# Four attention layers with a feed-forward: weighings in pairs, a rounded second product, shuffles out of PSUM, other places in the slots

## The reference

```python
# L0: layer norms, heads of 16, biases; then a feed-forward
x = x + softmax((ln(x) wq + bq)(ln(c) wk + bk)^T / 4) (ln(c) wv + bv) wo + bo
x = x + gelu(ln2(x) w1 + b1) w2 + b2            # 256 -> 1024 -> 256, exact gelu
# L1: heads of 64, rms norm of x, raw context, no scale
x = x + softmax((x * rsqrt(mean(x^2) + 1e-6) * nw wq)(c wk)^T) (c wv) wo
# L2: heads of 64, rotary embedding on q and k (pairs of neighbouring rows), mask, then layer norm
x = ln(x + softmax(where(mask, rope(x wq) rope(c wk)^T / 8, -1e9)) (c wv) wo) * gamma + beta
# L3: as L0, without the feed-forward
```

## Time and profile before

| | |
|---|---|
| median of three runs | 2268.0 us (2266.34 to 2273.81) |
| profiled execution, own time | 2268.11 us |
| its span | 2266.2 us |
| busy in the span: PE, PEld, DVE, ACT, POOL | 2062.2, 1678.8, 1425.7, 1263.5, 581.4 us |
| mean granted clock of TensorE | 0.963 |

### The profile page before, as it was taken

How to read it: one execution, slowest core, us unless ns; L and a number is a source line. 1 busy time by engine, 2 the same in 40 slices (tenths; PEclk the granted TensorE clock), 3 DMA queues, 4 the chain that set the end, 5 groups by cost and what they waited for, 6 DMA issues and landing times. The chain is left out here.

```text
span 2266.2 us, 50658 instructions
## 1 busy us (share of the span) xinstructions
PE 2062.2 (91%) x18696; PEld 1678.8 (74%) x18696; DVE 1425.7 (63%) x2880; ACT 1263.5 (56%) x3225; POOL 581.4 (26%) x676
## 2 busy tenths in 40 slices
PE   6888986979999999999989999899999998889897
PEld 5777775867787787787767777777777776777776
DVE  5777774335445455454587777777777775577775
ACT  3677774335555555555555555555555554577775
POOL 3232320000000000000055655655556551000000
PEclk8999997989999999999999999999999999799999
DMA  6444332011000000000001000000000000344432
GB/s 170 135 136 139 117 122 82 0 52 58 14 8 8 14 8 15 8 8 14 9 15 35 15 9 9 9 9 15 9 9 10 1 1 1 115 121 121 121 122 71
DMA packets 72965, 109.69 MB, mean 48 GB/s; under 512 B 7062, under 2 KB 62618, under 8 KB 72730
## 3 DMA queue, kind: packets, MB, share of 16 engines
q1 hardware_dynamic: 72442, 105.98, 15.4%
q10 hardware_dynamic: 288, 0.51, 0.1%
HBM read 69.28 MB, written 37.19 MB: 47 GB/s over the span
## 5 line engine op out<-in xcount | busy, mean ns | idle before, releaser
L1444 ACT ACTIVATE wide_P<-PS,MX 100x361 f32<-100x361 f32 x512 | 288.9, 564 | 415.3 <-DVE MX L1562 411.4
L1562 DVE TENSOR_REDUCE MX<-PS 100x2 f32<-100x722 f32 x256 | 231.5, 904 | 181.4 <-PE PS L1312 181.3
L626 ACT ACTIVATE L_P<-PS,MX 100x361 f32<-100x361 f32 x512 | 253.5, 567 | 132.2 <-DVE MX L752 132.2
L752 DVE TENSOR_REDUCE MX<-PS 100x2 f32<-100x722 f32 x256 | 219.9, 900 | 48.3 <-PE PS L512 47.7
L1738 POOL TENSOR_TENSOR wide_AC<-wide_T,wide_COSM 128x362 f32<-128x362 f32 x128 | 118.0, 922 | 409.4 <-DVE wide_SH L1520 408.1
L1335 PE MATMUL PS<-wide_PT,wide_V 128*64 128x100 f32 (+1 forms) x3072 | 189.1, 257 | 29.6 <-issue 29.6
L524 PE MATMUL PP<-CON,L_P 100*128 100x100 f32 x1536 | 183.9, 257 | 26.6 <-DVE L_PT L759 20.7
L1335 PEld LDWEIGHTS PS<-wide_PT,wide_V 128*64 128x64 f32 (+1 forms) x3072 | 139.4, 136 | 84.4 <-issue 68.2
L524 PEld LDWEIGHTS PP<-CON,L_P 100*128 100x128 f32 x1536 | 151.5, 144 | 47.8 <-ACT L_P L626 34.3
L1321 PE MATMUL PP<-CON,wide_P 100*128 100x100 f32 x1536 | 179.6, 254 | 0.8 <-ACT wide_PT L1451 0.5
L1321 PEld LDWEIGHTS PP<-CON,wide_P 100*128 100x128 f32 x1536 | 164.6, 144 | 10.4 <-issue 2.0
(11 more groups left out here) (255 smaller groups left out, 5434.4 us busy)
## 6 DMA issues: line engine op xcount, KB each, us to landing
strips<-L_KS SPq DMA_DIRECT2D x256, 90.5 KB
L_KA<-strips SPq DMA_DIRECT2D x64, 362.0 KB, 3.1
C<-ctx_t SPq DMA_DIRECT2D x32, 361.0 KB, 3.1
kept<-L_CTH SPq DMA_DIRECT2D x16, 361.0 KB, 4.9
kept<-L_CTL SPq DMA_DIRECT2D x16, 361.0 KB, 5.5
L_CTH<-kept SPq DMA_DIRECT2D x16, 361.0 KB, 4.3
L_CTL<-kept SPq DMA_DIRECT2D x16, 361.0 KB, 5.1
C<-in_ctx SPq DMA_DIRECT2D x16, 256.0 KB, 3.4
```

What stands on the lines that cost most here:

```text
L626: nc.scalar.activation(P[:, (4 * g + j) % 8, 0:SK], PSB[0:SQ, j, 0:SK], ACT.Exp, bias=MX[:, s % 2, 4 * q + j:4 * q + j + 1], scale=1.0).th ...
L752: nc.vector.tensor_reduce(MX[:, s % 2, 4 * q + 2 * i:4 * q + 2 * i + 2], PSB[0:SQ, 2 * i:2 * i + 2, 0:SK], AX.X, ALU.max, negate=True).the ...
L1444: nc.scalar.activation(P[:, (2 * g + i) % 4, 0:SK], PS_[i][0:SQ, 0:SK], ACT.Exp, bias=MX[:, s % 2, h:h + 1], scale=1.0, accum_out=DEN[:, s ...
L1562: nc.vector.tensor_reduce(MX[:, s % 2, 2 * p:2 * p + 2], PSB[0:SQ, 0:2, 0:SK], AX.X, ALU.max, negate=True).then_inc(Z["maxed"], 1)
```

## The change

- Narrow layers: ScalarE does job M ahead of the exponentials, VectorE job O ahead of the unload.
- Feed-forward: the output product is made transposed and in rounded halves (w2 and the hidden units split), unit by unit, two units behind the hidden product, with the bias b2 at the eviction; its result is turned back by TensorE. w1 is split in two parts. The loop is written out.
- Wide layers: one tile C for the raw context in place of two, so context s + 1 is loaded when that of s is split, and the first of these loads comes after those of L2's weights; the wait for w_o moves to the first projection. PT has six parts. Weighings g - 3 and g - 2 run together in odd slots. O moves from slot 3 to 5, V from slots 3, 4, 5 (and 5, 6, 7 behind the weighing) to 2, 3, 4 and 6, 7, 0.
- L2: VectorE swaps rows out of the PSUM bank, for keys right after the maximum; ScalarE's copy waits for the swap and GpSimd for the copy. The layer norm moves from slots 4 and 6 to 6 and 7. L2's output weights are loaded one entry later in SP's list.

The core of the diff (`turn`, `gain`, `stats`, `split` and `add` of the feed-forward are as before but for their indices; indentation is reduced):

```diff
-C = sb("C", [128, 2, KV_TILES, E])
+C = sb("C", [128, KV_TILES, E])
...
+        for key in a_:
+            if key[0] == "M":
+                job(key)
...
             exponential(g, 1)
         for key in a_:
-            job(key)
+            if key[0] != "M":
+                job(key)
...
         for key in a_:
-            if key[0] == "N":
+            if key[0] in "NO":
                 job(key)
         if turns:
             unload(g - 1)
         for key in a_ + b_:
-            if key[0] != "N":
+            if key[0] not in "NO":
...
+W1H, W1L = local("W1H", [128, KE, FF], f32r), local("W1L", [128, KE, FF], f32r)
+W2H, W2L = local("W2H", [128, nf, E], f32r), local("W2L", [128, nf, E], f32r)
...
+    def hidden(u):
+        i, t = divmod(u, nf)
+        pe.wait_ge(Z["w1_low"], 1 + 2 * t // nf)
+        pe.wait_ge(Z["y_low"], KE * (i + 1))
+        if u >= 2:
+            pe.wait_ge(Z["hid_taken"], u - 1)
+        c = slice(128 * t, 128 * t + 128)
+        todo = [x for k in range(KE) for x in ((W1H[:, k, c], YH[:, i % 2, k, :]), (W1H[:, k, c], YL[:, i % 2, k, :]),
+                                               (W1L[:, k, c], YH[:, i % 2, k, :]))]
+        for m, (x, y) in enumerate(todo):
+            last = nc.tensor.matmul(hid[u % 2][:, 0:GS], x, y, start=m == 0, stop=m == len(todo) - 1)
+        last.then_inc(Z["hid_made"], 1)
+    def output(u):
+        i, t = divmod(u, nf)
+        pe.wait_ge(Z["w2_low"], 1)
+        pe.wait_ge(Z["hid_low"], u + 1)
+        if t == 0 and i >= 2:
+            pe.wait_ge(Z["out_taken"], KE * (i - 1))
         for k in range(KE):
+            c = slice(128 * k, 128 * k + 128)
+            for m, (x, y) in enumerate(((W2H, HH), (W2H, HL), (W2L, HH))):
+                last = nc.tensor.matmul(outs[i % 2][k][:, 0:GS], x[:, t, c], y[:, u % 4, :], start=t == 0 and m == 0,
+                                        stop=t == nf - 1 and m == 2)
+        last.then_inc(Z["out_made"], 1)
...
+    def back(i, half):
+        pe.wait_ge(Z["out_taken"], KE * (i + 1))
+        if i + 2 < groups:
+            pe.wait_ge(Z["gained"], KE * (i + 2) + half + 1)
+        else:
+            pe.wait_ge(Z["added"], G * (i - 1) + 2 * half + 2)
+        for v in range(2):
+            g = 2 * half + v
+            for k in range(KE):
+                last = nc.tensor.transpose(turns[half][0:SQ, E * v + 128 * k:E * v + 128 * k + 128],
+                                           OT[:, k, SQ * g:SQ * g + SQ], ident)
+        last.then_inc(Z["back_made"], 1)
+    for k in range(KE):
+        turn(0, k)
+    for u, i, t in stream():
+        if u < U:
+            hidden(u)
+        if u >= 2:
+            output(u - 2)
+        if i + 1 < groups and t in (3, 4):
+            turn(i + 1, t - 3)
+        if 0 < i < groups and t in (5, 6):
+            back(i - 1, t - 5)
+    for half in range(2):
...
+    def split_w1(n):
+        act.wait_ge(w_in["ffn"][0], 16)
+        nc.scalar.activation(W1H[:, :, HALVES[n]], w1[:, :, HALVES[n]], ACT.Copy).then_inc(Z["w1_high"], 1)
...
+    def hidden(u):
+        act.wait_ge(Z["hid_made"], u + 1)
+        if u >= 3:
+            act.wait_ge(Z["hid_low"], u - 2)
+        nc.scalar.activation(H32[:, u % 3, :], hid[u % 2][:, 0:GS], ACT.Gelu, bias=col("b1", u % nf)).then_inc(Z["hid_taken"], 1)
+        act.wait_ge(Z["hid_taken"], u + 1)
+        if u >= 4:
+            act.wait_ge(Z["out_made"], u - 3)
+        nc.scalar.activation(HH[:, u % 4, :], H32[:, u % 3, :], ACT.Copy).then_inc(Z["hid_high"], 1)
+    def output(i):
+        act.wait_ge(Z["out_made"], nf * (i + 1))
+        if i:
+            act.wait_ge(Z["back_made"], 2 * i)
         for k in range(KE):
+            nc.scalar.activation(OT[:, k, :], outs[i % 2][k][:, 0:GS], ACT.Identity, bias=col("b2", k), scale=1.0).then_inc(Z["out_taken"], 1)
+    split_w1(0)
+    split_w1(1)
+    for k in range(KE):
+        gain(0, k)
+    act.wait_ge(wo_in["ffn"], 16)
+    nc.scalar.activation(W2H[:, :, :], w2, ACT.Copy).then_inc(Z["w2_high"], 1)
+    for u, i, t in stream():
+        if u < U:
+            hidden(u)
+        if i and t == 2 and i < groups:
+            output(i - 1)
+        if i + 1 < groups and t in (3, 4):
+            gain(i + 1, t - 3)
+    output(groups - 1)
...
+    def split_w1(n):
+        dve.wait_ge(Z["w1_high"], n + 1)
+        nc.vector.tensor_tensor(W1L[:, :, HALVES[n]], w1[:, :, HALVES[n]], W1H[:, :, HALVES[n]].bitcast(fp32),
+                                ALU.subtract).then_inc(Z["w1_low"], 1)
...
+    def hidden(u):
+        dve.wait_ge(Z["hid_high"], u + 1)
+        if u >= 4:
+            dve.wait_ge(Z["out_made"], u - 3)
+        nc.vector.tensor_tensor(HL[:, u % 4, :], H32[:, u % 3, :], HH[:, u % 4, :].bitcast(fp32), ALU.subtract).then_inc(Z["hid_low"], 1)
...
+    stats(0)
+    moments(0)
+    split_w1(0)
     normalise(0)
+    split_w1(1)
+    for k in range(KE):
+        split(0, k)
+    dve.wait_ge(Z["w2_high"], 1)
+    nc.vector.tensor_tensor(W2L[:, :, :], w2, W2H[:, :, :].bitcast(fp32), ALU.subtract).then_inc(Z["w2_low"], 1)
+    for u, i, t in stream():
+        if u < U:
+            hidden(u)
+        if i + 1 < groups:
+            if t == 0:
+                stats(i + 1)
+            elif t == 1:
+                moments(i + 1)
+            elif t == 2:
+                normalise(i + 1)
+            elif t in (4, 5):
+                split(i + 1, t - 4)
+        if 0 < i < groups and t in (5, 6):
+            add(i - 1, t - 5)
...
-after_scores, after_turn, after_weigh = [], [], []
+after_scores, after_turn = [], []
 if s + 1 < NS:
     after_scores.append(("K", s + 1, p))
 if s % 2 and s + 1 < NS:
...
     after_turn.append(("X", s + 2, 0))
 if p == 1 and s > 0:
     after_turn.append(("R", s - 1, 1))
-if p == 3 and s > 0:
+if p == 5 and s > 0:
     after_turn.append(("O", s - 1, 0))
 if p == 5 and s < NS:
     after_turn.append(("R", s, 0))
-if p in (3, 4, 5) and s < NS:
-    after_turn.append(("V", s, 3 + p - 3))
-if p in (5, 6, 7) and s + 1 < NS:
-    after_weigh.append(("V", s + 1, p - 5))
-return after_scores, after_turn, after_weigh
-
-SLOTS = [(s, p) for s in range(NS) for p in range(HP)] + [(NS, p) for p in range(4)]
+if p in (2, 3, 4) and s < NS:
+    after_turn.append(("V", s, 3 + p - 2))
+if p in (6, 7) and s + 1 < NS:
+    after_turn.append(("V", s + 1, p - 6))
+if p == 0 and 0 < s < NS:
+    after_turn.append(("V", s, 2))
+return after_scores, after_turn
+SLOTS = [(s, p) for s in range(NS) for p in range(HP)] + [(NS, p) for p in range(6)]
...
     context(0)
-    context(1)
...
-        if s + 2 < NS:
+        if s + 1 < NS:
             sp.wait_ge(Z["c_low"], KE * (s + 1))
-            context(s + 2)
+            context(s + 1)
...
+        if s == B + 1:
             sp.wait_ge(Z["added"], B)
...
         pe.wait_ge(Z["scaled"], 2 * (s + 1))
+        if s == 0:
+            pe.wait_ge(wo_in["L1"], 16)
...
-                                        PT[0:r, (2 * g + i) % 4, SQ * c:SQ * c + SQ], start=c == 0, stop=c == KV_TILES - 1)
+                                        PT[0:r, (2 * g + i) % 6, SQ * c:SQ * c + SQ], start=c == 0, stop=c == KV_TILES - 1)
...
-    pe.wait_ge(wo_in["L1"], 16)
...
-        if 2 <= g <= HP * NS + 1:
+        if g % 2 and 3 <= g <= HP * NS + 1:
+            weigh(g - 3)
             weigh(g - 2)
-        for key in after_weigh:
-            job(key)
...
-        act.wait_ge(Z["made"], job_no[key] + 1)
+        act.wait_ge(Z["shuffled"], r + 1)
         if r >= NT:
             act.wait_ge(Z["rotated"], r - NT + 1)
...
-        if g >= 2:
-            act.wait_ge(Z["weighed"], g - 1)
-        nc.scalar.activation(PT[:, (2 * g + 1) % 4, :], PP[1][:, 0:KV_TILES * SQ], ACT.Copy).then_inc(Z["unloaded_odd"], 1)
+        if g >= 3:
+            act.wait_ge(Z["weighed"], g - 2)
+        nc.scalar.activation(PT[:, (2 * g + 1) % 6, :], PP[1][:, 0:KV_TILES * SQ], ACT.Copy).then_inc(Z["unloaded_odd"], 1)
...
-        dve.wait_ge(Z["copied"], r + 1)
-        nc.vector.stream_shuffle(SH[:, r % NB, 0:n], T32[:, r % NT, 0:n], [q ^ 1 for q in range(32)]).then_inc(Z["shuffled"], 1)
+        dve.wait_ge(Z["made"], job_no[key] + 1)
+        nc.vector.stream_shuffle(SH[:, r % NB, 0:n], bank(key)[:, 0:n], [q ^ 1 for q in range(32)]).then_inc(Z["shuffled"], 1)
...
+        shuffles_first = s + 1 < NS and rope(s + 1)
+        if shuffles_first:
+            for key in after_scores:
+                job(key)
...
-        for key in after_scores:
-            job(key)
+        if not shuffles_first:
+            for key in after_scores:
+                job(key)
...
-            if p == 4 and s < NS:
+            if p == 6 and s < NS:
                 post_stats(s - 1)
-            if p == 6 and s < NS:
+            if p == 7 and s < NS:
                 post(s - 1)
...
-        pool.wait_ge(Z["shuffled"], r + 1)
+        pool.wait_ge(Z["copied"], r + 1)
...
-        if B < s < NS and p == 4:
+        if B < s < NS and p == 6:
```

(4 more changed lines are left out.)

241 lines of the change are left out of this document (97 added, 144 removed).

## The result

Median 2114.7 us (2111.77 to 2117.97) against 2270.7 us in the same runs: a ratio of 0.9315, interval 0.9291 to 0.9338, faster. The forecast was 2127 us, its range 2080 to 2185. Executed again among the last experiments, the changed kernel took 2118.1 us (2111.56 to 2119.25), ratio 0.9331 (0.9311 to 0.9352).

The account below looks back on a forecast made before the run. TensorE was taken as the busiest engine in every stage, short of work in different ways. Terms -38 (narrow layers), -17 (feed-forward), -2 (wide start), -24 (L1), -60 (L2) sum to -141: 2266.2 - 141 + 1.9 = 2127 us, range 2080 to 2185.

Parts of the forecast that it names:

- Narrow layers, -38: L0 and L3: moving job M's copy and job O's addition earlier returns two thirds of 57.8 us of weight-load waits.
- Feed-forward and start, -19 together: Feed-forward -17 from a cheaper second product and earlier row statistics; start of the wide layers -2.
- L1, -24: First wide layer: -19 from weighing in pairs, -5 from moving value products and O; ends -12 and -32.
- The pairs' step: Wide layers: a group of 24 weighing records takes 1.20 us, saving 0.30 us a pair, 64 pairs, -19 in L1.
- L2, -60: Second wide layer: -19 from pairs, -41 from idle and half-clock time coming back; ends -10 and -105.
- The step that the wait for the scaling goes: L2, slot 2: the weighing's 1.41 us wait for VectorE's scaling should vanish, with the weighing one slot later.
- what stays are slots 2, 3, 6 and 7, 7.4 of the 12.5 us: L2: context splitting and layer norm on VectorE keep about 0.9 us a slot of the loss per two entries.
- this loop keeps its 4.0 us: L2's light slots: swapping rows from PSUM leaves VectorE's loop unchanged, since ScalarE's order is as long as before.
- Rival 2: L2: clock stays high and nearly all of the 12.5 us returns, another 40 us less, 2087 us; chance 0.15.
- Rival 1: L2: stays held by VectorE's loop, clock goes on falling, gain 19 and little more, 2163 us; chance 0.19.
- Rival 4: Wide layers: pairing saves nothing, a 24-record group being no denser than two of 12; 2165 us; chance 0.07.
- Rival 3: L2: shuffles out of PSUM make the kernel slower than before, some 2310 us at 3.5 us each; chance 0.04.

Follow-up runs that it names:

- b1_values_moved: The kernel before with only the six value products moved to their new slots, ahead of the weighing; 2198.8 us, ratio 0.9698.
- e10_o_old: The changed kernel with only the projection O put back in slot 3; 2107.7 us, ratio 0.9281.
- e9_old_order: The changed kernel with single weighings two slots behind and V and O in their old slots, row swap out of PSUM kept; 2162.6 us, ratio 0.952.
- e2_single_lag2: The changed kernel with one weighing in every slot, two slots behind, instead of pairs; 2126.1 us, ratio 0.9377.
- c2_four: The changed kernel with O in slot 3, L2's last norm step later, second context loaded earlier, most L3 context loads and outputs through GpSimd's queue; 2093.8 us, ratio 0.9227.

## Why the prediction was right, and where its steps were wrong

The time lies 12 us from the forecast, but two large terms missed in opposite senses (narrow layers 13 to 15 us too much, L2 27 us too little), so part of that closeness is luck.

**Narrow layers, -38: mechanism right, size off.** 23 by stages (320.4 to 306.1 and 299.2 to 290.7, means of nine executions), 22 to 25 by undoing it. Two thirds of the 57.8 us that the weight loads waited was too much: TensorE's own idle time behind the two evictions was 43.3 us, and a little over half of it came back. The rest is not shown; the slot's own loop, which the prediction names, would fit. In L3 the DMA of the kept context took a small part of their place.

**Feed-forward and start, -19 together: right.** 91.4 us against "near 92", and 20 to 23 to L1's second entry. Its two main terms fit as well: from the first hidden product to TensorE's last instruction of the stage 96.2 us before and 80.6 after (forecast -15), from the first instruction of the stage to that product 12.9 and 9.3 (forecast -4.2). No experiment undid this part. The "+1.1 us" for the second context was 3.8 in one execution (ScalarE's wait for it) and nothing in the other, so its size is that of a transfer that lands now earlier, now later.

**L1, -24: near, its parts wrong.** It gave 20. The pairs' step was sized at 0.30 us from a group of 24 that should take 1.20 us. That group measured as forecast (1.26 busy, the next product 1.18 behind its start):

```profile
680.48 1.26 PE L1409 MATMUL PS<-wide_PT,wide_V 128*64 128x100 f32 x24
681.66 0.41 PE L1386 MATMUL PS<-wide_KH,wide_QH 64*100 64x362 f32 x2
```

What the saving is worth depends on the slot that the weighing leaves: 0.1 us a pair with O in slot 5, and from `b1_values_moved` to `e10_o_old` (607.6 to 595.5, single weighings to pairs, both with O in slot 3) 0.2, an upper value since other edits lie between them. The places of V and O together were sized at -5: V gave 15 (622.7 to 607.6), and O's move cost 6 to 7. The failing step is the reading of the earlier trace rows: "busy 43.10 of 43.1 us" was taken for a queue without slack. But a light slot's busy time has its products spread: in slot 0 of an even entry the six turns took 0.61 us to the next start with the weighing behind them, and 0.46 with a value product behind them, the same products with the same own time. Some 7 us come already from standing ahead of the weighing in the old slots (`e9_old_order`); the other 8 of V's 15 come with the two products that left slot 5. A value product costs about 1.0 us more in a light slot (3.43 to 4.45) and gives back 1.4 to 1.5 in slot 5.

**L2, -60: the sign of each part right, the sizes not.** It gave 87.

- The step that the wait for the scaling goes, since the weighing stands one slot later, was right: the kernels with pairs and V in the old slots have no such wait. A value product in front of the weighing removes it as well (`b1_values_moved` and `e2_single_lag2`, 2.9 and 2.8 us left). What failed is what its going was worth: with V in the old slots the idle time only moved to the scores, and L2 stayed at 695.4 us.
- The step "what stays are slots 2, 3, 6 and 7, 7.4 of the 12.5 us" failed: slot 3 of an odd entry was long through half clock (11.3 us at 0.73, then 8.8 at 1.00), not through VectorE's work. The values' move alone brings 58 us (737.9 to 680.1).
- The step "this loop keeps its 4.0 us" held for the light slots (4.00 us in slots 2 and 6 of an even entry). But the swap's gain was taken as nothing from it, and it is 39 us: VectorE's wait for the copy, 39.2 us in 450 of the kernel before (L1520, 72 times, at most 0.8), is time that it lacks in the slots with other work.
- The price of a shuffle from PSUM, taken as 0 from the earlier trace rows, is right (562 to 566 ns; the Trainium skill's 62 more cycles, "VectorE: DVE Perf Modes", The TRN2 errata, are not seen).
- The pairs, sized at 19 here, gave 2 to 3.

These gains do not add. V's places alone bring 58 us in L2. A kernel with the old slots and single weighings, but with the swap out of the bank, is 57 us below the kernel before (an upper value for the swap, as said there). Both together bring 84 (737.9 to 653.8). So how much of the 87 belongs to which depends on which is taken first.

**Rivals.** Rival 2 (the clock stays high, nearly all returns) is what L2 did: its mean clock is 1.00. Rival 1 fails: short idle times stayed in L2 (17 us in 651) and the clock did not fall, so the rule of the Trainium skill ("TensorE: Matmul & The Clock Gate", A second HAM failure mode) did not decide here. What went in front of the low clock before was, in the entry shown, an idle stretch of 1.85 us with another of 0.48 behind it. With V and O in the old slots 2.2 us idle in slot 0 of the even entries had a mean clock of 0.79 in slot 1 behind them; with single weighings the same entries idle 1.4 us in slot 1, and the mean clock of every slot stays at 1.00 (means of seven entries). Rival 4 is half true: the pairs save 8 to 11 us, not 38. Rival 3 fails by the 566 ns; its last figure was also summed wrongly, since by its own terms 3.5 us a shuffle would come to some 2370 us, not 2310.

Not tried: pairs alone and the swap alone in the kernel before, the value products ahead of the weighing in their old slots there, and each part of `c2_four` alone.

## What to carry to other kernels

Where a queue alternates light and heavy slots, first move independent products into the light ones, and in front of an instruction that waits: here that alone was worth 70 us of a change of 156, with no instruction saved. Merging groups pays only once the slot that they leave is filled; otherwise the same edit loses. For a value that two engines need from one bank, look at what each engine waits for, and try the order in which the busier one reads first: in L2 of the kernel before VectorE was busy 543 of 738 us and ScalarE 394, and VectorE was the one that waited. When two edits cure the same wait, measure each with and without the other, since their gains overlap.

## What had not been expected of the hardware

- One subtraction of 362 columns on VectorE, both operands in SBUF, had a mean of 606 or of 864 ns in the same stage, with the source and order of the row swap changed. Without a multiplication of GpSimd beside it, it took 524 to 527 ns in the changed kernel. The Trainium skill ("SBUF — State Buffer", Who interferes with whom) says that a VectorE instruction with two inputs in SBUF, as this one, contends with what GpSimd reads there; these numbers agree. Why one that lies wholly beside GpSimd's work took 576 ns in one order and 928 in the other is not shown.
- "Busy" of TensorE is no measure of slack: L1's busy time fell from 613.0 to 602.6 us by the value products' places alone, and to 591.5 in `e10_o_old`, which also has the pairs, with the same products.
- Six turns take 0.61 us up to the start of what follows when that is the weighing, whose products go to halves of the array, and 0.46 when it is a value product (slots 0, 2 and 6 of even L1 entries; `before`, `b1_values_moved`). That the change to the halves is the reason is not shown.
- The same narrow layer took 285.6 to 295.7 us in nine executions of the same instructions, while L1 and L2 repeated within 2 us.
